# A two-layer graph network kernel: native float32 products side by side, segment sums one step later, row stores first in the load queue

## The reference

```python
wk = relu(e @ k_w1 + k_b1) @ k_w2 + k_b2            # e: edge_attr_64, [E, 64]
wv = relu(e @ v_w1 + v_b1) @ v_w2 + v_b2
k = sum_s sh[:, s] * (x[src] @ Cqk[:, s, :]) * wk   # sh: edge_attr_9, [E, 9]; [E, 8 heads, 16]
v = sum_s sh[:, s] * (x[src] @ Cv[:, s, :]) * wv
attn = einsum('ehd,ehd->eh', q[dst], k)             # q = x @ Wq
ex = exp(attn - segment_max(attn, dst)[dst])
upd = segment_sum(v * ex / (segment_sum(ex, dst)[dst] + 1e-16), dst) @ W_out
x = layernorm(x + batchnorm(x @ W_self + upd))
agg = segment_sum(e, dst) / max(count, 1)           # second layer
out = layernorm(x + mlp3(concat([agg, x])))
```

## Time and profile before

| | before |
|---|---|
| median of three runs | 5016.33 us |
| the profiled execution | 5049.76 us |
| its span | 5047.8 us |
| mean granted TensorE clock | 0.975 |
| TensorE busy | 4772.7 us (95%) |
| VectorE busy | 4058.6 us (80%) |
| ScalarE busy | 3414.7 us (68%) |
| GpSimd busy | 3713.3 us (74%) |
| DMA, mean | 199 GB/s |

### The profile page before, as it was taken

The page is one execution under the profiler, slowest core; times in us unless marked ns, Lnnn a source line. Parts: engine busy times, 40 slices in busy tenths (PEclk is TensorE's granted clock), DMA queues, the critical chain, the costliest instruction groups (busy, mean ns, idle before and its releaser), DMA issues. The chain is left out here.

```text
span 5047.8 us, 115383 instructions
## 1 busy us (share of the span) xinstructions
PE 4772.7 (95%) x35582; PEld 4503.5 (89%) x35582; DVE 4058.6 (80%) x5044; ACT 3414.7 (68%) x6495; POOL 3713.3 (74%) x3494
## 2 busy tenths in 40 slices
PE   7999999999999999999999999999999999998256
PEld 6999999999999999999999999999999999998143
DVE  5888888888888888888888888888888888886435
ACT  2677677677777767767777677777777777776137
POOL 3777777777777777777777777777777777774460
PEclk9999999999999999999999999999999999998578
DMA  8899999999999999999999999999999999996220
GB/s 218 202 215 210 208 210 214 208 214 210 212 207 214 213 208 213 211 210 211 211 213 211 207 216 213 216 214 214 213 216 212 214 214 216 212 213 158 91 68 26
DMA packets 693458, 1006.45 MB, mean 199 GB/s; under 512 B 120054, under 2 KB 378168, under 8 KB 693160
## 3 DMA queue, kind: packets, MB, share of 16 engines
q1 hardware_dynamic: 574856, 753.93, 65.7%
q0 software_dynamic: 112960, 242.16, 22.7%
q10 hardware_dynamic: 5600, 9.83, 0.7%
HBM read 826.64 MB, written 178.93 MB: 199 GB/s over the span
## 5 line engine op out<-in xcount | busy, mean ns | idle before, releaser
L825 PE MATMUL psum<-chi,zhi 128*128 128x256 f32 x7840 | 2316.9, 301 | 2.2 <-DVE rv L731 2.1
L535 POOL DMA_INDIRECT gq<-qtab,idxs x1568 | 1881.1, 1200 | 478.0 <-issue 475.8
L828 PE MATMUL psum<-clo,zhi 128*128 128x256 f32 x7840 | 2144.4, 282 | 0.0
L530 POOL DMA_INDIRECT gx<-in_xg,idxs x1568 | 1555.4, 992 | 465.0 <-issue 453.5
L827 PE MATMUL psum<-chi,zlo 128*128 128x256 f32 x6272 | 1768.4, 282 | 0.0
L825 PEld LDWEIGHTS psum<-chi,zhi 128*128 128x128 f32 x7840 | 1478.6, 189 | 99.3 <-issue 99.3
L828 PEld LDWEIGHTS psum<-clo,zhi 128*128 128x128 f32 x7840 | 1476.2, 188 | 0.0
L827 PEld LDWEIGHTS psum<-chi,zlo 128*128 128x128 f32 x6272 | 1183.6, 189 | 93.0 <-issue 93.0
L685 DVE TENSOR_TENSOR z<-psum,shb 128x1536 f32<-128x1536 f32 (+1 forms) x784 | 1130.5, 1483 | 126.2 <-PE psum L797 118.7
L580 ACT ACTIVATE zhi<-z 128x1536 fp32r<-128x1536 f32 (+1 forms) x784 | 993.5, 1267 | 247.9 <-DVE z L685 244.0
L710 DVE TENSOR_TENSOR zlo<-z,zhi 128x1536 fp32r<-128x1536 f32 (+1 forms) x784 | 922.2, 1217 | 0.0
(11 more groups left out here) (210 smaller groups left out, 6335.1 us busy)
## 6 DMA issues: line engine op xcount, KB each, us to landing
shb<-in_shT SPq DMA_DIRECT2D x392, 640.0 KB
shb<-in_shT SPq DMA_DIRECT2D x392, 512.0 KB
rows<-ot SPq DMA_DIRECT2D x392, 416.0 KB
e<-in_eT SPq DMA_DIRECT2D x392, 128.0 KB
drow<-rankd SPq DMA_DIRECT2D x392, 128.0 KB
gx<-in_xg,idxs POOLq DMA_INDIRECT x1568
gq<-qtab,idxs POOLq DMA_INDIRECT x1568
qtab<-qs ACTq DMA_DIRECT2D x25, 256.0 KB, 5.7
```

What stands on the lines that cost most here:

```text
L530: nc.gpsimd.indirect_dma_start(out=gx[:, s, k, :], out_offset=None, in_=xg[:, :], in_offset=bass.IndirectOffsetOnAxis(ap=ids[:, k:k + 1], ...
L535: nc.gpsimd.indirect_dma_start(out=gq[:, s, k, :], out_offset=None, in_=qtab[:, :], in_offset=bass.IndirectOffsetOnAxis(ap=ids[:, TC + k:T ...
L825: mm(tpb[:, k, :], zhi[:, s, j, e], chi[:, j, :], start=(j == 0), stop=False)
L828: last = mm(tpb[:, k, :], zhi[:, s, j, e], clo[:, j, :], start=False, stop=(j == ST - 1))
```

## The change

It has these parts; line numbers are those of the kernel before.

- TensorE's step: `sums(a, 0)`, `turned_x(c)`, `hidden(c)`, `sums(a, 1)`, `tensor_products(t)`, `turned_features(c-1)` for odd c, `edge_weights(c)`, with a = t-7 instead of b = t-6.
- ScalarE's step: copies and maxima for a = t-7 in the new places, `hidden(c)` ahead of the first `z_first_part`, `hidden_first_part` between its two halves, and `segments(b)` instead of `segments(b+1)`, behind `feature_rows` and ahead of `count` and `find`.
- SyncE's step: `store(t-8)` first instead of `store(t-7)` last, `targets(t-5)` instead of `targets(t-4)`.
- One drain step more; chunk slots are unchanged.
- The backward scan reads the same tile of masks as the forward one, one element further, so that one mask DMA in four steps goes, and the padding DMA of the preparation.
- Tensors used only up to the loop are given back before the mending block, and the final block counts with three semaphores in place of seventeen, one for each engine, with thresholds for the same instructions.

```diff
@@ steps @@
-    for n in range(R0 + UN * TURNS, NC + LAG + 2):
+    for n in range(R0 + UN * TURNS, NC + LAG + 3):
@@ sync, masks @@
-                        for ahead, tile in ((0, nmf), (1, nmb)):
-                            src = newd[bass.ds(g.value() * CH + ahead, GT * P)].rearrange("(t e) -> t e", t=GT)
-                            sp.dma_start(tile[:, s, :], src.unsqueeze(1).broadcast_to([GT, H, P])).then_inc(nm_in[s], 16)
+                        src = newd[bass.ds(g.value() * CH, GT * P)].rearrange("(t e) -> t e", t=GT)
+                        sp.dma_start(nmf[:, s, 0:P], src.unsqueeze(1).broadcast_to([GT, H, P])).then_inc(nm_in[s], 16)
@@ sync, step @@
+                        if (t + (-LAG - 2)).there():
+                            store(t + (-LAG - 2))
                         if (t + 2).there():
                             harmonics(t + 2)
                         if (t.r + 3) % 2 == 0 and (t + 3).there():
                             features(t + 3)
-                        if (t + (2 - LAG)).there():
-                            targets(t + (2 - LAG))
+                        if (t + (1 - LAG)).there():
+                            targets(t + (1 - LAG))
                         g = t + (-2)
                         if g.r % GC == 0 and g.there():
                             masks(g)
-                        if (t + (-LAG - 1)).there():
-                            store(t + (-LAG - 1))
@@ scalar, step @@
-                        c, b = t + 1, t + (-LAG)
+                        c, b, a = t + 1, t + (-LAG), t + (-LAG - 1)
+                        if a.there():
+                            sums(a, 0)
+                        if t.there():
+                            edge_weights(t)
                         if b.there():
                             weights(b)
-                        if t.there():
-                            edge_weights(t)
+                        if c.there():
+                            hidden(c)
+                        if a.there():
+                            sums(a, 1)
+                            maxima(a)
                         if c.there():
                             z_first_part(c, 0)
-                            hidden(c)
+                            hidden_first_part(c)
                             z_first_part(c, 1)
-                            hidden_first_part(c)
                             if c.r % 2 == 1:
                                 feature_rows(c + (-1))
                         if b.there():
-                            sums(b, 0)
-                            maxima(b)
-                        if (b + 1).there():
-                            segments(b + 1)
-                        if b.there():
-                            sums(b, 1)
+                            segments(b)
@@ vector, segment_maxima @@
-                        v.tensor_tensor_scan(mr[:, ::-1], nmb[:, s, ::-1], mf[:, ::-1], -BIG, ALU.add, ALU.max).then_inc(mr_done, 1)
+                        v.tensor_tensor_scan(mr[:, ::-1], nmf[:, s, P:0:-1], mf[:, ::-1], -BIG, ALU.add, ALU.max).then_inc(mr_done, 1)
@@ tensor, step @@
-                        c, b = t + 1, t + (-LAG)
+                        c, a = t + 1, t + (-LAG - 1)
+                        if a.there():
+                            sums(a, 0)
                         if c.there():
                             turned_x(c)
                             hidden(c)
+                        if a.there():
+                            sums(a, 1)
                         if t.there():
                             tensor_products(t)
                         if c.there() and c.r % 2 == 1:
                             turned_features(c + (-1))
-                        if b.there():
-                            sums(b, 0)
                         if c.there():
                             edge_weights(c)
-                        if b.there():
-                            sums(b, 1)
@@ final block @@
-            SS = {k: sem(f"{k}_made") for k in ("r", "y", "dd", "sq", "lg", "rs", "x1", "s0", "h0", "h1", "y2", "dd2", "sq2",
-                                                "lg2", "rs2", "o")}
-            prod_made = sem("products_made")
+            MADE = {"pe": ("mean", "var", "z0", "z1", "z2", "mean2", "var2"),
+                    "act": ("r", "sq", "lg", "rs", "h0", "h1", "sq2", "lg2", "rs2"),
+                    "dve": ("y", "dd", "x1", "s0", "y2", "dd2", "o")}
+            made_by = {e: sem(f"blocks_made_by_{e}") for e in MADE}
```

More of the change, by code:

```diff
@@ L104, in gnn_kernel @@
     qtab = dram("qtab", (NP, O), fp32)
-    newd = dram("newd", (EP + P,), bf16)
+    newd = dram("newd", (EP,), bf16)
     chaind = dram("chaind", (EC,), fp32)
@@ L116, in sem @@
             return ctx.enter_context(nc.semaphore(name))
[L119 to L126, removed]
         wout = sb("wout", [O, 2, P])
@@ L151, in gnn_kernel, with eb @@
         banks = [psum[:, i * 512:(i + 1) * 512] for i in range(8)]
+        edges = ctx.enter_context(ExitStack())
+        def eb(name, shape, dt=fp32):
+            return edges.enter_context(nc.sbuf_tensor(name, shape, dt))
+        chi = eb("chi", [P, ST, KV], f32r)
+        clo = eb("clo", [P, ST, KV], f32r)
+        w1 = eb("w1", [P, 2, P])
+        b1c = eb("b1c", [P, 1])
+        w2hi = eb("w2hi", [P, KV], f32r)
+        w2lo = eb("w2lo", [P, KV], f32r)
+        b2hl = eb("b2hl", [P, KV], f32r)
+        ones = eb("ones", [P, P], f32r)
+        idx_all = eb("idx_all", [P, 2 * EC], i32)
+        ndcol = eb("ndcol", [P, EC])
         load = sem("load")
@@ L172, in gnn_kernel @@
             neg = ps("neg", [P, EC], bf16)
-            npad = ps("npad", [2, P // 2], bf16)
             nodei = ps("nodei", [P, NT + 1], i32)
@@ L220, in _ @@
                         sp.dma_start(dst, src).then_inc(load, 16)
-                    sp.wait_ge(neg_made, 3)
-                    sp.dma_start(newd[0:EP].rearrange("(p c) -> p c", p=P), neg[:, :]).then_inc(tables_stored, 16)
-                    sp.dma_start(newd[EP:EP + P].rearrange("(p c) -> p c", p=2), npad[:, :]).then_inc(tables_stored, 16)
+                    sp.wait_ge(neg_made, 2)
+                    sp.dma_start(newd.rearrange("(p c) -> p c", p=P), neg[:, :]).then_inc(tables_stored, 16)
                     sp.wait_ge(rank_made, 6)
@@ L229, in _ @@
                     sp.wait_ge(load, 16 * len(consts))
-                    sp.wait_ge(tables_stored, 64)
+                    sp.wait_ge(tables_stored, 48)
                 @block.tensor
@@ L306, in _ @@
                     v.memset(epsc[:, :], EPS)
-                    v.memset(npad[:, :], -BIG).then_inc(neg_made, 1)
                     dve.wait_ge(padded_made, 1)
@@ L318, in _ @@
                     v.tensor_tensor(same[:, :], dcur[:, :], dprv[:, :], ALU.is_equal).then_inc(neg_made, 1)
-                    dve.wait_ge(neg_made, 2)
+                    dve.wait_ge(neg_made, 1)
                     v.tensor_scalar(neg[:, :], same[:, :], 1.0, BIG, ALU.subtract, ALU.mult).then_inc(neg_made, 1)
@@ L378, in gnn_kernel @@
             drow = ms("drow", [P, 2, CH], bf16)
-            nmf = ms("nmf", [P, 2, P], bf16)
-            nmb = ms("nmb", [P, 2, P], bf16)
+            nmf = ms("nmf", [P, 2, P + 1], bf16)
             hid = ms("hid", [P, CH])
@@ L783, in _ @@
                     v.memset(shb[D:P, :, ST - 1, :], 0.0).then_inc(shb_zero, 1)
-                    dve.wait_ge(shb_zero, 1)
+                    v.memset(nmf[:, :, P:P + 1], -BIG).then_inc(shb_zero, 1)
+                    dve.wait_ge(shb_zero, 2)
                     steps(dve, step)
@@ L885, in _ @@
                     steps(pe, step)
+        edges.close()
         with ExitStack() as mend:
@@ L1085, in gnn_kernel @@
             st_d, st_a, st_pe = sem("stats_dve"), sem("stats_act"), sem("stats_pe")
-            SS = {k: sem(f"{k}_made") for k in ("r", "y", "dd", "sq", "lg", "rs", "x1", "s0", "h0", "h1", "y2", "dd2", "sq2",
-                                                "lg2", "rs2", "o")}
-            prod_made = sem("products_made")
-            PRODUCTS = ("mean", "var", "z0", "z1", "z2", "mean2", "var2")
+            MADE = {"pe": ("mean", "var", "z0", "z1", "z2", "mean2", "var2"),
+                    "act": ("r", "sq", "lg", "rs", "h0", "h1", "sq2", "lg2", "rs2"),
+                    "dve": ("y", "dd", "x1", "s0", "y2", "dd2", "o")}
+            made_by = {e: sem(f"blocks_made_by_{e}") for e in MADE}
             def wait_made(engine, name, i, j):
[L1093 to L1096, removed]
+                for e, names in MADE.items():
+                    if name in names:
+                        engine.wait_ge(made_by[e], (i * len(names) + names.index(name)) * GN + (j + 1))
             with ExitStack() as fin1:
@@ L1275, in turn @@
                             for j in range(GN):
-                                sp.wait_ge(SS["o"], i * GN + (j + 1))
+                                wait_made(sp, "o", i, j)
```

(14 more changed lines are left out.)

8 lines of the change are left out of this document (3 added, 5 removed).

## The result

| | before | after |
|---|---|---|
| median | 5016.91 us (5014.75 to 5021.02) | 5200.38 us (5198.74 to 5202.28) |
| the profiled execution | 5049.76 us | 5201.75 us |
| mean granted TensorE clock | 0.975 | 0.976 |

The ratio is 1.0365 (95% interval 1.0347 to 1.0383): 183 us slower, where 178 were forecast. That is closer than its terms deserve; three of them were off and cancel, as the experiments show.

A forecast was written before the change was run, and what follows sets the result against it. TensorE, busy 95% of the span, was taken as the bound. New waits +214, gather waits -33 and tail -3 gave +178 us on 5016, so 5194 us; own range 5141 to 5323, stated range 5105 to 5285.

The forecast's parts named there:

- The step that decided: TensorE's first sums of a step: wait for ScalarE's `seg`, held behind `feature_rows`, in every step with L813, mean 1.11 us.
- The wait, +214: TensorE before the first sums: 193 waits for `seg` of 1.11 us mean, 214 us in total.
- The gather waits, -33: TensorE's transposes of gathered rows: longer steps remove 27.1 us of idle time and three half-clock stretches, -33 us.
- Memory moved: 0: Tensors at other addresses in the changed kernel: claimed to cost or gain nothing, 0 us.
- Seams: TensorE's changes between native float32 and float32r matmuls: 392 fewer, worth 0 to 4 us, taken as 0.
- tail: Drain after the last tensor product: seven steps instead of six, some shorter, together -3 us, between -8 and +8.
- edits with one answer: Stores, segment numbers, mask load, scans' odd pitch, fewer semaphores: each 0 or hidden, at most about 5 us.
- Half clock after each wait: Rival: each new TensorE wait drops the clock to 1.2 GHz, 328 us more, 5522 us; chance 0.05.
- Faster: Rival: `seg` ready at TensorE's first sums, chain from L813 below 2.33 us, only gains stay, 4979 us; chance 0.10.
- Nothing measurable: Rival: a wait of 0.2 us, 39 us, against gains of 37; 5016 us, +-10; chance 0.03.

The follow-up runs named there:

- e1: Kernel after, with ScalarE making `seg` (`segments(b)`) before it copies the feature rows; 4952.43 us, ratio to before 0.9862.
- e4: Kernel before with only the new step orders on TensorE, ScalarE and SyncE and the extra drain step; 5247.20 us, ratio 1.0451.
- e11: e4 with `seg` made ahead of the feature rows, the exchange of e1; old masks, layout and counting; 5021.77 us, ratio to before 1.0001.
- e3: Kernel before with `hidden(c)` ahead of `turned_x(c)` in TensorE's step; 5017.21 us, ratio 0.9997.
- e5: e4 plus the single tile of masks in place of two; 5192.36 us, one execution.
- e8: e4 plus an unused tensor of 516 bytes behind the two mask tiles; 5184.38 us, one execution.
- e2: Kernel before with only the new memory layout: product constants and index tables allocated behind the other constants; 5028.89 us, ratio 1.0013.
- e6: e4 plus the final block's counting by three semaphores in place of seventeen; 5246.03 us, one execution.
- e7: e4 plus the new layout, loop weights and index tables behind the constants; 5250.42 us, one execution.
- e9: Kernel before plus an unused tensor of 32 bytes, putting `zhi` and `zlo` on a multiple of 64; 5077.92 us, ratio 1.0102.
- e12: e9 plus `hidden` ahead of the x transposes, the swap of e3; 5013.65 us, ratio to before 0.9928.

## Why the prediction was right, and where it wasn't

**The step that decided was right.** The wait stands before the first sums of a step, in every second step and in no other (167 of 332 in the middle stretch), released by `seg`, in a fixed chain L818, L597, `far`, `seg`. TensorE is idle 1.11 us in the row above. The mean step is 12.017 us (forecast 12.1), the busy share of the middle stretch 96%. VectorE's wait for `hidhi` went and brought nothing. e1 takes the cause away, not its effect, and the loss goes.

**The wait, +214: mis-sized, by a price that I took from the wrong row.** The chain on ScalarE was forecast to end 3.34 us behind the start of L818 and ends 3.22 behind it (3004.62-3001.40), as `far` begins 0.49 instead of 0.60 behind L597. But I let TensorE start 0.05 behind `seg`, from a drain step. In the row above it starts 0.38 behind it (3005.00-3004.62). In the trace the wait for `seg` is there an instruction of its own on TensorE's queue, and two register and semaphore instructions for the next waits follow it at 3004.76 and 3004.90, before the weights load at 3004.99. Over the middle stretch there are two kinds of wait. In 126 of 167 the start comes 0.33 to 0.38 behind `seg`, with two instructions in between. In the other 41, every fourth, the wait for `seg` is the last instruction ahead of the weights load, and the start comes 0.10 behind it; these are the 41 that the view puts down to "issue". Measured from L818, the sums start at 3.51 in the mean instead of 3.39. Mean price of a wait: 1.17 us by e4 and e11, 1.23 by the starts in after (3.51; less 2.38, which is the forecast's 2.33 and 0.11 more in every second; and 0.10 for the slower sums), against 1.11: 12 to 23 us more than forecast.

**The gather waits, -33: wrong in size, against the median.** I took 27.1 us of idle time and three stretches at half clock from the profiled execution, which was 33 us above the median of its kernel, and subtracted them from the median. The waits do go, but e3 shows that their going is worth nothing there (0.9997). I had noted that the profiled run was 0.7% above the median, and drew no consequence from it.

**"Memory moved: 0": wrong by 47 us.** The step failed where I costed the removed mask tile by its DMA alone. The pitch of the tensor products fell from 120.0 ns (e4) to 117.8; that alone is 56 x 2.2 ns x 392 = 48 us. e4 without the moved tensors takes 5247.20 us, with them (e5, e8) 5192 and 5184, the whole change 5200.38. Had the addresses stayed, the change would have cost some 230 us (e4).

**Seams, tail and edits with one answer, 0, -3 and 0: right together.** e11 holds all of the new orders, the drain step with them, and is at 1.0001; the layout alone and the counting alone show next to nothing (e2 1.0013; e6 and e7 within 4 us of e4, one execution each). The single terms weren't separated.

So 5194 was to be raised by 12 to 23 and by 33, and lowered by 47: 5192 to 5203, measured 5200.38. The nearness of the forecast is owed to terms that cancel; that the change is slower, and by what, isn't.

**The rivals.** *Half clock after each wait*: no. The granted clock is 1.00 over the middle stretch, without a stretch at half clock; the 167 idle times of 0.7 to 1.1 us in it left the clock alone. The two stretches at half clock that after has in its loop, at 124 and 168 us, follow gather waits of 3.78 and 1.49 us in the first steps. By the Trainium skill, page "TensorE: Matmul & The Clock Gate", section "A second HAM failure mode: psum-queue depth-cycling", frequent small idles could have made it swing; the trace of after does not agree. In e9, with gather waits of up to 4.1 us, it did fall, 19 times. *Faster*: its point was a chain from L818 to `seg` of under 2.33 us; it is 3.22. The gain that it named (4979) is passed by e1 only with the quicker matmuls; without them, in e11, there is no gain. *Nothing measurable*: no.

## What to carry to other kernels

When a product moves ahead in an engine's step, look at what makes its operand: instructions that are ready must not stand behind one that waits for the present step, and exchanging two calls was worth 226 us at the same pitch (e4 to e11), 248 in the changed kernel. A term that is read from one profiled execution may be subtracted from a median only after asking whether that median contains it. When tensors are removed or added, the start addresses of all behind them move; compare the pitch of the main loop's matmuls before and after, and try a pad of 32 or 64 bytes. Then look at the time too: e9 has the quicker matmuls and is the slower kernel.

## What the runs showed of the hardware

- The pitch of float32r products of 256 columns hangs on where the loop's tensors start: 119.8 to 120.0 ns with `zhi` and `zlo` 32 bytes beyond a multiple of 128 or on one, 117.8 and in some steps 113.4 on an odd multiple of 64; 96 bytes beyond wasn't tried. An unused tensor moved the whole by 1.2% (e4 to e8). Steps with 113.4 are none in after and e9, a sixth in e5 and e8, a quarter in e1 and a third in e12. Which tensor it is, and why some steps have 113 ns, stays open.
- Behind the end of the work that TensorE waits for, the first matmul comes 0.33 to 0.38 us later where two further instructions stand between the wait and the weights load (126 of 167 waits in after), and 0.10 later where none does (41); in the drain it was 0.05. Nobody tried here to put the wait last on purpose.
- 392 fewer changes between native float32 and float32r products, with all else that is new in the orders, make no difference that can be measured (e11, 0.9991 to 1.0011).
- A gather of GpSimd takes 0.95 us to issue, and 1.36 and 2.07 in the two rows in which it begins during `zlo`, a VectorE instruction with two inputs in SBUF; the mean of the 335 that do so in before is 1.85.
